# A three-stage audio tower on one core: a third buffer for packed expert tiles, and a new order of the work in a step

## What is computed

```python
h = segment_attention(x[::2 of each segment])            # softmax(x x^T / 16) x, per block of 128
a = layernorm(h)
q, k, v = silu(conv4(a @ Wq)), silu(conv4(a @ Wk)), silu(conv4(a @ Wv)); beta = sigmoid(a @ Wb)
delta   = delta_rule(l2norm(q), l2norm(k), v, beta)      # chunks of 32: T = inv(I + A), then a running state S
short, long = conv3(v), conv63(v)
w = softmax(mlp([a, statistics of short, long, delta, v]) / temp)          # 4 heads x 4 branches
o = rmsnorm(w0*short + w1*long + w2*delta + w3*v)
h = h + o @ Wo
y = layernorm(h)
route = top 2 of 6 experts by a quantised projection of y, weights by a softmax of the two
out = h + sum over the two experts of weight * gelu(y @ w1[e]) @ w2[e]
```

## Time and profile before

| what | value |
| --- | --- |
| median of 3 runs | 2990.84 us |
| the 3 runs | 2976.18, 2990.84, 2993.9 us |
| the profiled execution | 3000.57 us |
| its span, first to last instruction | 2998.9 us |
| granted TensorE clock, mean over the span | 0.855 |
| busy: PE, DVE, ACT, POOL | 2337.4, 1803.2, 1354.4, 981.0 us |

### The profile page before, as it was taken

One profiled execution on the slowest core, in us unless ns is written; L12 is line 12 of the kernel. 1 busy time (PEld: TensorE's weight loads), 2 busy tenths in 40 slices (PEclk: granted clock), 3 DMA queues, 4 the chain that ended last, 5 costly groups with the idle time before them and its releaser, 6 DMA issues.

```text
span 2998.9 us, 60224 instructions
## 1 busy us (share of the span) xinstructions
PE 2337.4 (78%) x21042; PEld 1775.0 (59%) x21042; DVE 1803.2 (60%) x5204; ACT 1354.4 (45%) x2784; POOL 981.0 (33%) x797
## 2 busy tenths in 40 slices
PE   6999999989877778777877787787788787866640
PEld 4666666658755566565656555665566566655430
DVE  5999999969646555555555565554556455441001
ACT  4888888853423324333433344344344444432210
POOL 1444444440002222222333333433433333342014
PEclk9999999987778777888888889888898989986665
DMA  3777777787843344566556654655555465445544
GB/s 103 250 239 241 243 239 234 237 273 267 344 138 136 130 161 152 183 211 220 197 187 226 232 186 155 207 187 183 171 195 187 145 210 195 164 134 181 164 148 126
DMA packets 361962, 583.47 MB, mean 195 GB/s; under 512 B 133470, under 2 KB 274878, under 8 KB 352190
## 3 DMA queue, kind: packets, MB, share of 16 engines
q1 hardware_dynamic: 338910, 507.24, 51.5%
q0 software_dynamic: 20448, 59.79, 5.6%
q10 hardware_dynamic: 2304, 12.58, 1.0%
HBM read 369.39 MB, written 277.48 MB: 216 GB/s over the span
## 4 chain that ended last, share of the span: by engine, by line
issue 23%; PE 14%; DMA 12%; POOL 11%; SPq 5%; DVE 4%; ACT 3%; another core or an unknown queue 0%; POOLq 0%; DVEq 0%; ACTq 0%
DMA rows<-v_all,posi 8%; POOL G L2582 6%; SPq L1534 2%; PE bank L1761 2%; DMA toeplitz<-v_all,posi 2%; POOL v_all L2543 2%; DMA wp<-wpack 2%; PE bank L1722 1%; POOL rows L2570 1%; PE bank L1648 1%; POOL v_all L2548 1%; PE bank L1878 1%; SPq L1568 1%; SPq L1558 1%; PE bank L1706 1%
## 5 line engine op out<-in xcount | busy, mean ns | idle before, releaser
L798 DVE SCALAR_TENSOR_TENSOR Y<-bank,convw,Y 128x383 f32<-128x383 f32 (+2 forms) x576 | 330.2, 601 | 4.3 <-ACT Y L686 4.0
L1878 PE MATMUL bank<-wp,he 128*128 128x256 f32 x504 | 200.5, 537 | 125.7 <-ACT he L2003 122.7
L2391 DVE SCALAR_TENSOR_TENSOR v_all<-G,wk,v_all 128x256 f32<-128x256 f32 x192 | 98.8, 555 | 313.5 <-DMA v_all<-h2s 244.3
L504 PE MATMUL bank<-pb,wqkv 128*128 128x384 f32 x768 | 283.9, 493 | 1.8 <-DVE Y L798 1.8
L2570 POOL DMA_INDIRECT rows<-v_all,posi x144 | 164.2, 1141 | 313.3 <-DMA rows<-v_all,posi 298.8
L1761 PE MATMUL bank<-v_all,w1g 128*128 128x384 f32 x512 | 229.9, 580 | 1.0 <-ACT v_all L1987 0.9
L1867 PE MATMUL bank<-ypT,wp 128*128 128x128 f32 x1008 | 160.8, 308 | 88.8 <-DMA wp<-wpack 75.9
L2543 POOL TENSOR_TENSOR v_all<-v_all,WT 128x768 f32<-128x768 f32 x32 | 72.1, 2254 | 437.3 <-DVE WT L2227 437.3
L1878 PEld LDWEIGHTS bank<-wp,he 128*128 128x128 f32 x504 | 118.3, 260 | 155.2 <-ACT he L2003 134.8
L2582 POOL DMA_INDIRECT G<-rows,posi x144 | 153.0, 1063 | 168.1 <-DVE v_all L2391 129.1
L1867 PEld LDWEIGHTS bank<-ypT,wp 128*128 128x128 f32 x1008 | 137.7, 212 | 111.4 <-DMA wp<-wpack 91.9
(11 more groups left out here) (258 smaller groups left out, 6083.0 us busy)
## 6 DMA issues: line engine op xcount, KB each, us to landing
wp<-wpack SPq DMA_DIRECT2D x252, 256.0 KB
packa<-pa SPq DMA_DIRECT2D x32, 1932.0 KB, 6.2
v_all<-packa SPq DMA_DIRECT2D x32, 1932.0 KB
rows<-toeplitz SPq DMA_DIRECT2D x16, 2496.0 KB, 10.7
packb<-pb SPq DMA_DIRECT2D x32, 768.0 KB, 6.2
v_all<-packb SPq DMA_DIRECT2D x32, 768.0 KB, 9.9
yp<-rows SPq DMA_DIRECT2D x192, 128.0 KB
rows<-op SPq DMA_DIRECT2D x192, 128.0 KB
```

The lines of the kernel that those rows point to most:

```text
L504: mm = pe.matmul(proj_bank[j][:, 0:T], wqkv[:, a, j * P:(j + 1) * P], xnT[:, a, :], start=(a == 0), stop=(a == HALF - 1), skip_group_check ...
L798: dve.scalar_tensor_tensor(out=Y[:, j, lag:T], in0=proj_bank[j][:, 0:T - lag], scalar=convw[:, j, CK - 1 - lag:CK - lag], in1=Y[:, j, lag: ...
L1878: mm = pe.matmul(bank[7][:, t * D:(t + 1) * D], he[:, t, :], wp[p % 2][:, t, HALF * DE:], start=True, stop=True)
L2391: dve.scalar_tensor_tensor(out=hc[:, b, :], in0=G[:, k, b, :], scalar=wk[:, c, k, b:b + 1], in1=hc[:, b, :], op0=ALU.mult, op1=ALU.add).th ...
```

## The change

It does the following:

- `yp` and `wp` get three buffers instead of two (`RING`); their loads are issued one slot further ahead. The first slot of a group is one later. `G` and `op` no longer have memory of their own; they lie in the buffer of systems group 2.
- Group 2 of the systems is solved wholly in the middle stage and stored there by POOL; group 3 is solved in steps 0 to 14 instead of 6 to 20 and stored in step 20.
- The gate's `gate_out` and `fold_gate` stand ahead of `merge_d` and `updates` on PE, and `exp_gate` ahead of `copy_merge_d` on ACT.
- `exp_routes` and `routing_weights` are done for batch `f` instead of `e`, one step later. `rank_routes` to `count` stand together, behind the mixture's sums.
- Many other calls of `step(i)` change places on all engines. On SP the residual for a batch is loaded in the step of its gather, and `load_u` stands at the end of the step.

```diff
+RING = 3
...
-SPLIT = 20
...
-            free = max(free, self.base(self.last[g] + 3) + 5)
+            free = max(free, self.base(self.last[g] + 3) + 6)
...
-            i = max(i, next(s for s in range(3 * NB) if self.base(s + 1) > out) + 1)
+            s = next(s for s in range(3 * NB) if self.base(s + 1) > out)
+            i = max(i, s if s < NB and out <= self.base(s) + 1 else s + 1)
...
+                pool.wait_ge(solve["step"], 3 * SOLVE_STEPS)
+                pool.dma_start(systems[2], X[2][:, :, :, :]).then_inc(solve["stored"], 16)
...
-                for j in range(1, SPLIT):
+                for j in range(1, SC - 1):
...
+        late = Region(X[2][:, :, :, :].rearrange("p s j i -> p (s j i)"))
+        G = late.take(2 * BLK, D).rearrange("p (k b) n -> p k b n", k=2)
+        op = [late.take(2, D) for s in range(2)]
...
-        yp_loaded = [signal(f"yp_loaded{s}", 32) for s in range(2)]
-        wp_loaded = [signal(f"wp_loaded{s}", 32) for s in range(2)]
+        yp_loaded = [signal(f"yp_loaded{s}", 32) for s in range(RING)]
+        wp_loaded = [signal(f"wp_loaded{s}", 32) for s in range(RING)]
...
-        yp = [sb(f"yp{s}", [P, 2, D]) for s in range(2)]
-        wp = [sb(f"wp{s}", [P, 2, EW]) for s in range(2)]
-        op = [sb(f"op{s}", [P, 2, D]) for s in range(2)]
+        yp = [sb(f"yp{s}", [P, 2, D]) for s in range(RING)]
+        wp = [sb(f"wp{s}", [P, 2, EW]) for s in range(RING)]
...
-        G = sb("G", [P, 2, BLK, D])
...
-                    if p > 1:
-                        sp.wait_ge(*pt_ready.now(p - 2))
+                    if p >= RING:
+                        sp.wait_ge(*pt_ready.now(p - RING))
...
-                    if p > 1:
-                        sp.wait_ge(*po_ready.now(p - 2))
+                    if p >= RING:
+                        sp.wait_ge(*po_ready.now(p - RING))
                     sp.wait_ge(*table_step.now(pairs[p][0]))
                     for t in range(2):
                         row = tile(p, t, 1)
-                        sp.dma_start(wp[p % 2][:, t, :], dram["wpack"][bass.ds(row, DE), :]).then_inc(wp_loaded[p % 2].sem, 16)
+                        sp.dma_start(wp[p % RING][:, t, :], dram["wpack"][bass.ds(row, DE), :]).then_inc(wp_loaded[p % RING].sem, 16)
...
                     n, it, e, f = i, i - 1, i - 2, i - 3
                     if n == 4:
                         sp.wait_ge(solve_stored, 16 * 2)
-                    if n == 10:
-                        store_solved(2)
                     if n == 14:
+                        sp.wait_ge(solve_stored, 16 * 3)
+                    if n == 20:
+                        store_solved(3)
+                    if n == 22:
                         sp.wait_ge(late_stored, 16)
-                    if n == 22:
-                        store_solved(3)
-                        sp.wait_ge(late_stored, 16 * 2)
                     k = plan.base(i)
-                    if i - 1 in plan.gathered_in:
-                        load_residual(plan.gathered_in[i - 1])
                     if 0 < it < NB:
                         load_h(sp, it)
                     store_tiles(k)
-                    load_expert(k + 2)
-                    load_tokens(k + 3)
+                    load_expert(k + 3)
+                    load_tokens(k + 4)
                     if 0 <= e < NB:
                         store_residual(e)
                     store_tiles(k + 1)
-                    load_expert(k + 3)
-                    load_tokens(k + 4)
+                    load_expert(k + 4)
+                    load_tokens(k + 5)
                     if i - 1 in plan.gathered_in:
                         store(plan.gathered_in[i - 1])
...
+                    if i in plan.gathered_in:
+                        load_residual(plan.gathered_in[i])
                     store_tiles(k + 2)
-                    load_expert(k + 4)
-                    load_tokens(k + 5)
-                    if 0 <= n < NB - 2:
-                        sp.wait_ge(*w_ready.now(n))
-                        load_u(sp, n + 2, n % 2)
+                    load_expert(k + 5)
+                    load_tokens(k + 6)
                     if i < (SETS - 1) * FILLS:
                         fill(i)
                     for q in range(3, plan.width(i)):
                         store_tiles(k + q)
-                        load_expert(k + q + 2)
-                        load_tokens(k + q + 3)
+                        load_expert(k + q + 3)
+                        load_tokens(k + q + 4)
+                    if 0 <= n < NB - 2:
+                        sp.wait_ge(*w_ready.now(n))
+                        load_u(sp, n + 2, n % 2)
...
+                    transpose_tokens(k + 1)
...
-                    transpose_tokens(k + 1)
+                    hidden(k + 1, e - 1)
                     if 0 <= e < NB:
                         project_out(e)
                     if 0 <= n < NB:
                         products(n, n % 2, 2)
-                    hidden(k + 1, e - 1)
+                    expert_out(k + 1)
                     if 0 <= it < NB:
+                        gate_x(it, it % 2, 0)
                         transpose_stats(it)
-                        gate_x(it, it % 2, 0)
                     if 0 <= n < NB:
                         merge_a(n)
-                    expert_out(k + 1)
                     if 0 <= it < NB:
...
-                    if 0 <= n < NB:
-                        merge_c(n)
-                    transpose_tokens(k + 2)
...
-                        merge_d(n, n % 2)
+                        merge_c(n)
+                    if 0 <= it < NB:
+                        gate_out(it)
...
                         fold_gate(it)
+                    if 0 <= n < NB:
+                        merge_d(n, n % 2)
                     if 0 <= e < NB:
                         route(e)
+                    if 0 <= n < NB:
+                        updates(n, n % 2, 0)
+                    hidden(k + 2, e)
                     if 0 <= n < NB:
                         state_update(n, n % 2, 0)
                     if 0 <= e < NB:
                         match_anchors(e)
                     if 0 <= n < NB:
...
-                    hidden(k + 2, e)
-                    if 0 <= n < NB:
                         kb_state(n, n % 2, 1)
...
-                    if 0 <= e < NB:
-                        ranks(e)
...
+                    if 0 <= e < NB:
+                        ranks(e)
                     expert_out(k + 3)
...
+                    if p == 0:
+                        act.wait_ge(solve_stored, 16 * 3)
...
-                    n, it, e = i, i - 1, i - 2
...
-                    if 0 <= n < NB:
+                        exp_gate(it)
+                    if 0 <= n < NB:
+                        copy_merge_d(n)
                         copy_update(n, 0)
                     if 0 <= e < NB:
                         squash(e)
-                    if 0 <= it < NB:
-                        exp_gate(it)
-                    if 0 <= e < NB:
-                        exp_routes(e)
...
-                    copy_out(k + 3)
                     if 0 <= it < NB:
                         squares(it)
+                    copy_out(k + 3)
...
+                def residual_stats(it, s):
                     dve.wait_ge(*h2_ready.now(it))
...
-                    if n < 6:
-                        at = SPLIT + min(3 * n, 5 + n)
-                        return 2, at, at + (3 if n < 2 else 2 if n == 2 else 1)
-                    at = 1 + 2 * (n - 6)
-                    return 3, at, at + 2
+                    return 3, 1 + 2 * n, 3 + 2 * n

                 def solve_columns(n):
-                    if n > 20:
+                    if n >= (SC - 2) // 2:
...
+                        combine(c, 1)
+                    if 0 <= e < NB:
+                        residual(e, e % 2)
                     if 0 <= n < NB:
                         mask(n, 4)
                         mask(n, 5)
                         transpose_diagonal(n, n % 2, 0, 0, n // 2).then_inc(tdiag_ready.sem, 1)
                     if 0 <= e < NB:
-                        residual(e, e % 2)
-                    if c is not None:
-                        combine(c, 1)
-                        combine(c, 2)
...
                         gate_logits(it)
+                    if 0 <= f < NB:
+                        routing_weights(f)
+                    if 0 <= it < NB:
                         gate_weights(it)
                         weigh(it, it % 2, 2)
                     if 0 <= n < NB:
                         state(n, 0)
...
-                    if 0 <= n < NB:
-                        input_stats(n, 5)
-                    if 0 <= e < NB:
-                        rank_routes(e)
-                    if 0 <= n < NB:
-                        delta_out(n, n % 2, 0)
-                        remainder(n, 1)
-                    if 0 <= it < NB:
-                        weigh(it, it % 2, 1)
-                    if 0 <= e < NB:
```

(17 more changed lines are left out.)

80 lines of the change are left out of this document (42 added, 38 removed).

## The result

The changed kernel takes 2770.19 us (2762.63 to 2774.79, 4 runs) where the kernel before takes 2984.8 us on the same chip: ratio 0.9278, 95% interval 0.9239 to 0.9317. The forecast was 2773 us. The profiled execution spans 2773.1 us, 225.8 us less than the one of before.

What follows compares the result with a forecast made beforehand. PE was taken as nearest to a bound, busy 79% of the last stretch with 12.2 us idle a step. Terms summed to −218 us from the profiled 3000.57, 2782.6, and 2773 us after the 9.7 us offset; range 2685 to 2880.

Steps and rivals of the forecast that it cites:

- Softmax a step later: Each late step: PE's 4.1 us wait of the third pair's expert_out for its gelu goes.
- Gate ahead of merges: Each late step: 1.5 us before kb_state go; updates waits 0.5 us behind ACT's copies of merge_d, between 0 and 1.5.
- Ranks: Each step: PE waits 1.8 us more at ranks, DVE's 3.4 us against PE's 0.7 and 1.0; bounds 0 and 3.1.
- Clock: Each step: the 1.2 GHz stretch behind the two idles goes, 2.6 us less; the one at the step's border stays.
- Rival B: Steps: both half-clock stretches go, as PE's longest idle is below 2 us; another 94 us less, 2679 us; chance 0.13.
- Residual +1.0: Each step on SP: load_u right in front of load_h, which residual needs, costs 1.0 us, between 0 and 5.7.
- rival C: Each step: SP comes so late to load_h that residual and gate_x wait; slower, 3056 us; chance 0.03.
- The 1.3 given back: Late steps: allowance because a walk misses waits, turning the sum of −8.3 us a step into −7.0.
- Systems, 0: Middle stage: group 2's 14.0 us of added columns are hidden by PE's convolution; cost 0, between 0 and 4 us.
- Steps 2 to 17, −30 and −60: Steps 2 to 7 gain 5.0 us each, 30 in all; steps 8 to 17 gain 6.0 each, 60 in all.
- Third buffer and tail, −24: Tail: 13.6 us of op waits, 5.0 of combine waits and a 12.3 gather go; an extra pair costs 6.8.
- Rivals C and D: C: steps slower by late load_h, 3056 us, chance 0.03. D: step changes cancel, about 2980 us, chance 0.03.

Runs made afterwards that it cites:

- soft_alone: The kernel before with only exp_routes and routing_weights moved one step later, exp_routes ahead of exp_gate: 2932.0 us, ratio 0.989.
- soft_back: The changed kernel with ranks early, and exp_routes and routing_weights put back in the step of their ranks: 2719.1 us, ratio 0.910.
- ranks_early: The changed kernel with rank_routes to count back behind routing_logits on DVE, and PE's ranks behind the second block's outputs: 2591.7 us, ratio 0.874.
- ring2: The changed kernel with two buffers for rows and weights instead of three, each pair loaded one slot later: 2752.1 us, ratio 0.929.
- combo_act: The changed kernel with ranks early, the solve's split as before, and pairs' stores from step 32 issued by ACT's queue: 2526.3 us, ratio 0.853.

## Why the prediction came out, step by step

The number is right within 3 us, and that closeness is luck: several terms of the sum are wrong, and they cancel. What is right is the mechanism of the late steps, that four waits go and a smaller one comes, and their idle time.

- **Softmax a step later, −4.1.** The wait is gone as said. By itself the part brings 1.2 us a step (soft_alone); undone where the other waits are gone, it costs 4.3 to 5.2 (soft_back against ranks_early). "A walk misses waits" was the right caution for the part alone.
- **Gate ahead of merges, −1.5 +0.5.** Sizes right: 1.35 a step back at `kb_state` when undone, 0.6 at `updates`, so `exp_gate` ahead of `copy_merge_d` holds PE up by no more than that. No net gain in time is shown.
- **First half, −2.1 −1.3.** Both waits are gone; the part was not undone by itself.
- **Ranks, +1.8.** The wait measures 1.6 (22.9 us in 14 steps); the recorded addends, 3.4 less 0.7 and 1.0, make 1.7. The price was mis-sized: the term priced the wait and not the clock behind it, 4.6 to 5.5 us in all.
- **Clock, −2.6.** This failed. The stretch behind the old gelu stall did go, and so did the wait of `products` (3.03 us in the row above) behind which the stretch at the border had stood. But the new wait at `ranks`, in this kernel together with a longer one at `q_state`, put a longer stretch there, 10 to 14 us, and the clock is 0.88 after 0.89. Rival B, which kept the clock high, describes ranks_early and not this change: I had counted the idle of 1.8 us as harmless because it was below the 4 us of the old one.
- **Shared port.** I added nothing for `weigh(it, 1)` moving up to where POOL multiplies. It took 0.95 us before and takes 1.78 in the changed kernel, in all 14 steps (before, then changed):

```profile
L2236 DVE TENSOR_TENSOR v_all<-first_stage,WT 128x768 f32<-128x768 f32 x14 | 13.3, 950 | 0.0
L2240 DVE TENSOR_TENSOR v_all<-first_stage,WT 128x768 f32<-128x768 f32 x14 | 24.9, 1775 | 0.4
```

  The rule of the Trainium skill that I had set aside ("SBUF — State Buffer", on the shared port pair) agrees with this row. In return the second instruction of `rank_routes`, 1.55 us in the earlier trace rows, takes 0.26, so on DVE nothing is lost in sum. The longer `weigh` stands right ahead of `remainder` and `delta_out`, for which the second `q_state` waits 0.9 us a step.
- **Residual +1.0.** No wait of `residual` for `load_h` shows; rival C found nothing in the profile. The 1.3 given back were needed for `q_state` instead: 37.8 us in 14 steps, 2.7 a step, against 0.85.
- **Systems, 0.** In the profiled pair right (+1.0), but only since both convolutions ran at the low clock. At the full one the term is 20 us, outside my bounds of 0 to 4. I took the cover from one profile whose clock was 0.78, so that the term came out is luck.
- **Steps 2 to 17, −30 and −60.** They gave 46 and 100. I scaled the step's gain down for them without a row that said so; the waits that the step's sum names were as large in the ten steps 8 to 17 as later, and one went that the forecast did not count, the wait for the weights. Before, in those steps:

```profile
PE bank L1878 <- ACT he L2003: 41.2, 10, 4.2
...
PE bank L1867 <- DMA wp<-wpack: 14.1, 9, 2.9
```

  ring2 shows that the second comes back without the third buffer, so the buffer did more here than the prediction gave it. PE's busy time fell as well, from 474.5 to 456.0 us.
- **Steps 0 and 1, 0.** Lost 11.4 us, at a clock of 0.57 instead of 0.72.
- **Third buffer and tail, −24.** Gave 10. One gather fewer at the end is there (9.8 us). The other terms stood at −11.8 (−13.6 − 5.0 + 6.8) and gave −0.2: 33 pairs in 255.6 us after 32 in 255.8. With the extra pair at its 6.8 us, half of SP's 27.3 us and all of the 5.0 brought 7 instead of 18.6, since SP still waits 20.0 us in this stretch: 10.1 for `op` and 9.9 for the landing of a result, which is new. That SP's issue is the bound was right (combo_act).
- **Rivals C and D.** Their prices, 3056 and 2980 us, take only the steps and leave out the tail (−24) and step 22 (−6) that the sum has. Neither came, so nothing hangs on it.

So the misses cancel: 56 us too little for steps 2 to 17, against 22 too much for steps 18 to 31 with step 22 (104 said, 82 given), 14 for the tail and 12 for the start.

## What to carry to other kernels

Price a new short wait on PE by what the granted clock does behind it, not by its own length: here 1.7 us cost 4.6 to 5.5, and idle matmuls in it bought back 4%. A stall removed alone shows only the difference to the next one; removed last, it shows its full price and the clock's (1.2 against 4.3 to 5.2 us a step here). Before calling work hidden, check at which clock its cover ran in the profile, since a cover that is slow in one run is short in the next.

## What the runs showed of the hardware that I had not expected

The granted clock stays at 0.50 for about 10 us behind idles of 2.15 and 1.73 us although PE is busy for 90% of that time, and with a filler of 1.56 us it is 0.99 over the 14 steps. Kernels with the same convolution have it at 0.78 or at 0.99, in 146 or 117 us, in one profiled execution each. A DVE multiplication of 128x768 takes 1.78 us beside a POOL multiplication and 0.95 without one. The third `q_state` waits 1.4 to 3.6 us in some kernels on two of the chips, where the same order waits 0.85 on the others.
